# Graph attention and feed-forward on one core: SyncE takes two transfers from GpSimd, and GpSimd's gathers are written out with their own waits

## The chip, the cores and the metric

The kernel runs on one core of a Trainium2 chip. The time is what the device needs for one execution, in microseconds (us), as the median of several runs. The core has five engines that run their own instruction streams and wait for each other by semaphores: TensorE (PE, with its weight loads as PEld), VectorE (DVE), ScalarE (ACT), GpSimd (POOL) and SyncE (SP). SP only issues DMAs; POOL issues DMAs too, among them the indirect ones that gather rows by index.

## The reference, cut to what matters

```
x: 12500 x 256;  src, dst: 212500 edges, sorted by dst (100000 each way and 12500 self loops)
x = x + gnn(layernorm(x), edges)
  gnn: h = x @ W (4 heads of 64);  alpha = leaky_relu(a_src[src] + a_dst[dst])
       alpha = softmax of alpha over the edges of each dst
       out = relu(layernorm(sum over edges of alpha * h[src] + bias))
x = x + ffn(layernorm(x))
  ffn: router on the mean row picks 2 of 8 experts for all rows;
       gelu(x @ W1) @ W2 of the two, weighted, then a layer norm
```

## The kernel before, in words

**Table.** The rows of x are taken in 50 pairs of 128-row blocks. For each pair PE transposes, multiplies with W and the attention vectors, ACT scales, and SP stores 269 values a row into `table` in DRAM (`store_pair`, L516). Beside it POOL gathers 75 groups of 128 rows of x straight from the input (`gather_x`, L712): the source rows of tile 13 of the first 75 edge chunks. It stages them in SBUF and stores them, three groups at a time, as `x_src` (`store_x`, L723). One group in three waits for an older store, since the staging space is a ring.

**Chunk loop.** The edges stand in 119 chunks of 14 tiles of 128. For chunk n POOL gathers the table rows of its source nodes, 128 rows with each indirect DMA (L775), into one of four slots of `rows`. In the first 73 of these steps that is 13 gathers, as tile 13 is computed from `x_src` by PE and ACT (SP loads it as `xe`, L554); in the other 46 it is 14. The indices come through `idx`, four slots, loaded by SP (L539), the first four by POOL (L737). Behind the gathers a chain over all engines computes maxima, weights and messages and adds them up by node. The chain for chunk n begins with ACT's copy of the gathered logits into `asrc` (L1130), followed by PE's matmul "lT" (L888); the two next chunks are gathered meanwhile.

Every engine runs the same step list, `walk`: six steps written out at the start, then loops of four steps. POOL's `walk` has four more written steps where the count of gathers changes.

**Waits.** In each step POOL waits until the slot's old content has been used: for `idx`, for ACT ("msgs") and DVE (the last message), and for PE ("expand*"). Before the seventh gather (t = `FIRST_ROW` = 6) it waits for PE's "lT^" of an earlier chunk. The last wait of each group is carried by a 1x1 `tensor_tensor` on `turn` (L768, L774), which also counts `s_turn`; in the x phase a `tensor_tensor` on `x_turn` (L711) does the same. `hold` is a semaphore increment that carries a wait of its own.

**Feed-forward.** After the last chunk the two experts are loaded and 25 groups of rows pass through PE, ACT and DVE. POOL is idle there.

The order of all this is written by hand; no scheduler sets it. The functions that the change touches, with the lines of the profile:

Of the kernel before, what the change touches and what calls it, by code (L numbers as in the profile page):

```python
# [128 lines left out]
def build(nc, x, src_t, dst, W, att_src, att_dst, g_bias, g_gamma, g_beta, Wr, br, W1, b1, W2, b2,  # L129
# [29 lines left out]
    with ExitStack() as ctx:  # L159
        def sb(name, shape, dt=F32):  # L160
            return ctx.enter_context(nc.sbuf_tensor(name, shape, dt))

        def sem(name):
            return ctx.enter_context(nc.semaphore(name))
# [37 lines left out]

        spare = sb("spare", [1, TILES], I32)
        turn = sb("turn", [1, 3])
        x_turn = sb("x_turn", [1, X_CHUNKS])
# [119 lines left out]
        s_wide = sem("s_wide")  # L325
        s_narrow = sem("s_narrow")
        s_dst16 = sem("s_dst16")
        s_first_idx = sem("s_first_idx")
# [4 lines left out]
        s_xidx = sem("s_xidx")  # L333
        s_xrow = [sem(f"s_xrow{i}") for i in range(RING - 1)]
        s_xsrc = [sem(f"s_xsrc{i}") for i in range(RING - 1)]
        s_xe = [sem(f"s_xe{i}") for i in range(2)]
        s_mid = sem("s_mid")
        s_fwr = sem("s_fwr")
# [90 lines left out]
        def hold(eng, counted):  # L429

            eng.sem_inc(counted, 1)  # L431

        def walk(eng, total, step, long=False, late=0):
            for j in range(-4, 2):
                step(At(0, RING, j), -j, 5)

            def four(k, late=RING):
                for j in range(RING):  # L440
                    step(At(k, RING, j + 2), -2, 5 if j < late else 2)

            with nc.Fori(0, X_ROUNDS, engines=[eng.engine], hint_back_edge=long) as k:
                four(k)
            hold(eng, s_nested)
            if late:
                four(X_ROUNDS, late)
            with nc.Fori(X_ROUNDS + (late > 0), SURE, engines=[eng.engine], hint_back_edge=long) as k:
                four(k, 0)
            hold(eng, s_nested)  # L450
            with eng.If(total > SURE * RING + 3):
                with eng.Fori(SURE, (STEPS - 3) // RING, WALK) as far:
                    with eng.If(far * RING + 3 < total):
                        with nc.Fori(far, far + WALK, engines=[eng.engine], hint_back_edge=long) as k:
                            with eng.If(k * RING + 3 < total):
                                four(k, 0)
                        hold(eng, s_nested)

        def among(lo, hi):

# [6 lines left out]
        def each_pair(begin, end):  # L467

            return [At(p // PAIR_RING, PAIR_RING, p % PAIR_RING) for p in range(begin, end)]

        def stored_x(eng):

            for i in range(RING - 1):
                eng.wait_ge(s_xsrc[i], 16 * len(x_parts[i::RING - 1]))
                hold(eng, s_nested)

        def rows_landed(at, lead, hi):

# [11 lines left out]
        def _(sp):  # L490
# [103 lines left out]
            hold(sp, s_sp_held)  # L594
            sp.dma_start(dst16[0:P * EP].rearrange("(p e) -> p e", p=P), narrow).then_inc(s_dst16, 16)
            pairs(SCHED_AT[1], PAIRS // PAIR_RING * PAIR_RING)
            for at in each_pair(PAIRS // PAIR_RING * PAIR_RING, PAIRS):
                pair(at, False)
            store_pair(each_pair(PAIRS - 1, PAIRS)[0], 0)
            total = steps_to_run(sp)  # L600
            sp.wait_ge(s_dst16, 16)
            hold(sp, s_sp_held)
            for j in range(2):
                load_dst(j, sp.value_load(step_tab[0:1, 1, j:j + 1], min_val=0, max_val=chunks - 1))
            for j in range(PAIR_RING):
                sp.wait_ge(s_tab[j], 16 * (len(range(j, PAIRS, PAIR_RING)) + 1))
                sp.wait_ge(s_x[j], 16 * len(range(j, LOADED, PAIR_RING)))
# [70 lines left out]
        def _(pool):  # L678
# [18 lines left out]
            def stage(c):  # L697
                c %= x_ring * X_BATCH
                return (c // X_SLOT + 1) * slot_size + c % X_SLOT * D

            def gather_x(c):

                i, r = divmod(c, X_BATCH)
                if r == 0 and i >= x_ring:
                    j = i % (RING - 1)
                    pool.wait_ge(s_xsrc[j], 16 * len(range(j, i - 1, RING - 1)))
                    hold(pool, s_granted)
                if c > 1:
                    pair_of = (c - 2) * 2 // 3
                    p1_pe.wait(pool, "T*", each_pair(pair_of, pair_of + 1)[0])  # L710
                    pool.tensor_tensor(x_turn[:, c:c + 1], zeros[0:1, 0:1], zeros[0:1, 0:1], ALU.add)  # L711
# [3 lines left out]
                if r == X_BATCH - 1 and i > 0:  # L715
                    store_x(i - 1)

            def store_x(i):

                j, part = i % (RING - 1), x_parts[i]  # L720
                pool.wait_ge(s_xrow[j], 16 * sum(p.stop - p.start for p in x_parts[j:i + 1:RING - 1]))
                hold(pool, s_granted)
                pool.dma_start(x_src.rearrange("(q i) d -> q (i d)", i=X_CHUNKS)[:, part.start * D:part.stop * D],  # L723
                               flat_rows[:, bass.ds(stage(part.start), (part.stop - part.start) * D)])\
                    .then_inc(s_xsrc[j], 16)

            pool.wait_ge(s_xidx, 16)
            for c in range(X_CHUNKS // 3):
                gather_x(c)
            pool.wait_ge(s_wide, 16)  # L730
            pool.tensor_scalar(narrow, wide, float(TOP16), None, ALU.min).then_inc(s_narrow, 1)
            for c in range(X_CHUNKS // 3, X_CHUNKS - 6):
                gather_x(c)
            total = steps_to_run(pool)
            for j in range(RING):
                c = pool.value_load(step_tab[0:1, 1, j:j + 1], min_val=0, max_val=chunks - 1)
                pool.dma_start(idx[j][:, :], src_t[bass.ds(c * P, P), :]).then_inc(s_first_idx, 16)  # L737
            for c in range(X_CHUNKS - 6, X_CHUNKS):
                gather_x(c)
            store_x(len(x_parts) - 1)  # L740
            pool.wait_ge(s_first_idx, 16 * RING)
            for j in range(RING):
# [5 lines left out]
            def gather(at, lo, hi):  # L748

                slot = at.slot(1)  # L750
                if not among(lo, hi)[3]:
                    return
                if at.off + 1 == 1:
                    stored_x(pool)
                pool.wait_ge(s_idx[slot], at.landed(1, 1))
                hold(pool, s_granted)
                first_row = lo == 1
                if not first_row:
                    act2.wait(pool, "msgs", at, -3)
                    hold(pool, s_granted)  # L760
# [1037 lines left out]
```

## Time and profile before

| | |
|---|---|
| median of 3 runs | 2975.58 us (2974.57 to 2977.32) |
| the profiled execution's own time | 2978.09 us |
| its span | 2976.4 us |
| mean granted clock of PE over the span | 0.86 |
| PE busy | 2415.0 us, 81% |
| DVE busy | 2279.3 us, 77% |
| ACT busy | 1725.7 us, 58% |
| POOL busy | 1694.2 us, 57%, of it 1524.3 in 1593 table gathers (L775), 957 ns each |

Busy time leaves out register, branch and semaphore instructions. The span is what the profiler saw from the first to the last instruction; the execution's own time is a little longer. In a row of the timeline the number in square brackets is the idle time of the engine before the instruction, and what ended it; "issue" is time in which it waited for nothing that the profile shows. An engine's share of the whole span says little here, since the stages have different limits.

### The profile page before, as it was taken

Reading aid. Unit: us, or ns where it says so; the run is one execution under the profiler, and the core shown is the slowest. Engines: PE = TensorE matmul, PEld = TensorE weight load, DVE = VectorE, ACT = ScalarE, POOL = GpSimd, SP = SyncE. Lnnn points to the kernel's source line nnn. Section 1 sums busy time; section 2 is a strip of 40 time slices with the busy share of each in tenths; the row PEclk is TensorE's granted clock in tenths of the full one; section 3 lists DMA queues with packets and bytes.
Section 4 is the critical chain, followed back from the end, with each engine's and each line's share of the span. In section 5 each row is a group of like instructions: output and inputs, shape, how many; then the busy total and the mean of one; then the engine's idle time right before and its main releaser. Section 6 shows DMA issues by size and latency. Waiting matters only on the chain. (4 is left out here: it accounts for less than half of the span.)

```text
span 2976.4 us, 67870 instructions
## 1 busy us (share of the span) xinstructions
PE 2415.0 (81%) x13182; PEld 1788.0 (60%) x13182; DVE 2279.3 (77%) x9533; ACT 1725.7 (58%) x5721; POOL 1694.2 (57%) x2041
## 2 busy tenths in 40 slices
PE   7927788888888888887777766777767999999998
PEld 6725566666666666665555555555554666667666
DVE  5638888988989989988888888888875565665655
ACT  4627777777777778777666666666662121221221
POOL 6777777777777777777777777777740000000000
PEclk9959888887878888878777787777778999999999
DMA  8966565656666655665555555555541111101101
GB/s 280 358 180 170 165 174 167 174 167 172 169 170 171 172 168 171 170 169 166 159 162 159 159 156 157 160 160 160 157 113 43 43 36 35 43 29 43 43 28 39
DMA packets 237752, 417.88 MB, mean 140 GB/s; under 512 B 68257, under 2 KB 153121, under 8 KB 237537
## 3 DMA queue, kind: packets, MB, share of 16 engines
q0 software_dynamic: 82640, 239.20, 30.3%
q1 hardware_dynamic: 153546, 175.16, 18.1%
q10 hardware_dynamic: 1351, 1.63, 0.2%
q14 instruction: 200, 1.64, 0.2%
q8 instruction: 15, 0.25, 0.0%
HBM read 362.57 MB, written 53.26 MB: 140 GB/s over the span
## 5 line engine op out<-in xcount | busy, mean ns | idle before, releaser
L775 POOL DMA_INDIRECT rows<-table,idx x1593 | 1524.3, 957 | 448.9 <-issue 386.4
L868 PE MATMUL bank<-msg,oh 128*128 128x260 f32 x3332 | 967.8, 452 | 2.2 <-ACT acc L1144 2.2
L868 PEld LDWEIGHTS bank<-msg,oh 128*128 128x128 f32 x3332 | 757.7, 232 | 147.5 <-DVE r_d L1492 2.6
L1098 ACT ACTIVATE msg<-rows,we 128x65 f32<-128x65 f32 x1904 | 478.5, 333 | 0.4
L916 PE MATMUL bank<-ident_b,ohT 128*128 128x128 bf16 x1680 | 190.0, 300 | 322.3 <-ACT oh L1091 126.5
L1398 DVE TENSOR_TENSOR msg<-rows,bank 128x520 f32<-128x520 f32 x595 | 382.7, 678 | 1.0 <-DVEq L110 0.8
L916 PEld LDWEIGHTS bank<-ident_b,ohT 128*128 128x128 bf16 x1680 | 159.8, 139 | 340.6 <-ACT oh L1091 201.2
L1233 ACT ACTIVATE msg<-bank,b_sb 128x512 f32<-128x512 f32 (+1 forms) x200 | 134.4, 678 | 365.5 <-PE bank L972 347.7
L985 PE MATMUL bank<-rows,msg 128*128 128x256 f32 x1536 | 340.6, 378 | 0.0
L972 PE MATMUL bank<-rows 128*128 128x512 f32 x768 | 335.5, 594 | 4.3 <-DMA rows<-in_L_ffn_W 4.3
L985 PEld LDWEIGHTS bank<-rows,msg 128*128 128x128 f32 x1536 | 288.4, 189 | 51.4 <-issue 10.6
L972 PEld LDWEIGHTS bank<-rows 128*128 128x128 f32 x768 | 146.0, 190 | 179.6 <-issue 175.5
L1118 ACT ACTIVATE carry<-bank 1x265 f32<-1x265 f32 x118 | 45.1, 382 | 311.2 <-PE bank L941 309.5
L1091 ACT ACTIVATE oh_b<-bank 128x896 bf16<-128x896 bf16 x238 | 205.3, 914 | 20.6 <-ACTq L110 15.6
L1091 ACT ACTIVATE oh<-bank 128x896 f32<-128x896 bf16 x238 | 200.7, 890 | 0.3 <-ACTq L110 0.2
L1393 DVE TENSOR_SCALAR ohT<-dst_b,node 128x896 bf16<-128x896 int16 x240 | 161.9, 674 | 8.0 <-DVE mtile L1511 7.4
L1500 DVE TENSOR_REDUCE node_v<-bank 128x70 f32<-128x210 f32 x119 | 44.5, 374 | 157.7 <-PE bank L888 157.5
L1669 DVE TENSOR_TENSOR rows<-bank,msg 128x512 f32<-128x512 f32 x49 | 31.6, 686 | 140.6 <-PE bank L985 137.6
L1180 ACT ACTIVATE selfm<-tab_w,ws 128x65 f32<-128x65 f32 x476 | 127.0, 338 | 3.9
L888 PE MATMUL bank<-ident,asrc 128*70 128x128 f32 x240 | 51.8, 298 | 94.7 <-ACT asrc L1130 78.7
L1148 ACT ACTIVATE r_c<-carry,r_f 1x65 f32<-1x65 f32 x476 | 125.0, 333 | 0.0
L1233 ACT ACT_TABLE_LOAD x12 | 15.4, 1283 | 183.3 <-PE bank L972 183.3
(223 smaller groups left out, 3957.3 us busy)
## 6 DMA issues: line engine op xcount, KB each, us to landing
dst_b<-dst SPq DMA_DIRECT2D x122, 448.0 KB
rows<-table,idx POOLq DMA_INDIRECT x1593
tab_w<-table SPq DMA_DIRECT2D x121, 134.5 KB
x_w<-in_x_rows SPq DMA_DIRECT2D x121, 128.0 KB
x_mid<-x_o SPq DMA_DIRECT2D x119, 128.0 KB
table<-msg SPq DMA_DIRECT2D x50, 269.0 KB, 5.2
rows<-x_mid SPq DMA_DIRECT2D x26, 512.0 KB, 3.5
msg<-in_x_rows SPq DMA_DIRECT2D x51, 256.0 KB
```

The costliest lines, as they stand in the source:

```text
L775: pool.indirect_dma_start(rows[:, slot, t, :], None, table, bass.IndirectOffsetOnAxis(ap=idx[slot][:, t:t + 1], axis=0), bounds_check=None ...
L868: mm = pe.matmul(psA, oh[:, of, t, :], msg[:, of, t, :], start=(t == 0), stop=(t == TILES - 1))
L916: mm = pe.transpose(ps[:, c:c + P], ohT[:, s, t, 0:P], ident_b[:, :])
L972: mm = pe.matmul(u, w1_sb[:, e, k, fk * P:(fk + 1) * P], fxT[:, at.slot(), k, :], start=(k == 0), stop=(k == KD - 1))
L985: mm = pe.matmul(psY[q // 2][:, q % 2, :], hT[:, f, q * P:(q + 1) * P], w2_sb[:, e, fk, :], start=(f == 0), stop=(f == 2 * KF - 1))
L1091: ins = act.activation(to[:, i * half:(i + 1) * half, :], psO[i].rearrange("p (t n) -> p t n", n=P), ACT.Copy)
L1098: ins = act.activation(head_cols(msg[:, s, t, :])[:, h, :], head_cols(rows[:, at.slot(), t, 0:HC1])[:, h, :], ACT.Copy, scale=we[:, t, h:h ...
L1148: ins = act.activation(head_cols(r_c[:, :])[:, h, :], head_cols(carry[:, 0:HC1])[:, h, :], ACT.Copy, scale=r_f[:, h:h + 1])
L1180: ins = act.activation(head_cols(selfm[:, :])[:, h, :], head_cols(tab_w[:, at.slot(), 0:HC1])[:, h, :], ACT.Copy, scale=ws[:, h:h + 1])
L1233: act3.mark(HID[f], act.activation(hT[:, f, 0:n], psU[f % len(psU)][:, 0:n], ACT.Gelu, bias=b1_sb[:, e, fk:fk + 1]))
L1393: return dve.tensor_scalar(ohT[:, s, t, 0:P], dst_b[:, s, :].rearrange("p (t n) -> p t n", n=P)[:, t, :], node[:, s:s + 1], None, ALU.is_e ...
L1398: mark(own, name, lambda: dve.tensor_tensor(msg[:, s, t:t + 2, :].rearrange("p t (h c) -> p t h c", h=H), rows[:, s4, t:t + 2, 0:HC1].rear ...
```

## The change

- SP, not POOL, loads the first four `idx`: right behind the loop over the pairs of blocks, before the last three table stores.
- SP, not POOL, stores the last three groups of x rows (semaphore `s_xlast`), behind the first loads of dst.
- POOL's `tensor_tensor` on `turn` and `x_turn` go. The gather behind it carries the wait itself.
- POOL's steps are written out one by one (`for n in range(-4, SURE * RING + 2)`), so that the values waited for are constants. Only steps beyond the first 119, which this input does not need, stay in a loop, with `turn` as before (`repeated`).

The other engines keep `walk`; its form with four written steps is gone, which only POOL used.

```diff
         def stored_x(eng):
             for i in range(RING - 1):
-                eng.wait_ge(s_xsrc[i], 16 * len(x_parts[i::RING - 1]))
+                eng.wait_ge(s_xsrc[i], 16 * len(x_parts[:-1][i::RING - 1]))
                 hold(eng, s_nested)
+            eng.wait_ge(s_xlast, 16)
+            hold(eng, s_nested)
...
             pairs(SCHED_AT[1], PAIRS // PAIR_RING * PAIR_RING)
+            total = steps_to_run(sp)
+            for j in range(RING):
+                c = sp.value_load(step_tab[0:1, 1, j:j + 1], min_val=0, max_val=chunks - 1)
+                sp.dma_start(idx[j][:, :], src_t[bass.ds(c * P, P), :]).then_inc(s_idx[j], 16)
             for at in each_pair(PAIRS // PAIR_RING * PAIR_RING, PAIRS):
                 pair(at, False)
             store_pair(each_pair(PAIRS - 1, PAIRS)[0], 0)
-            total = steps_to_run(sp)
...
                 load_dst(j, sp.value_load(step_tab[0:1, 1, j:j + 1], min_val=0, max_val=chunks - 1))
+            for j in range(RING - 1):
+                sp.wait_ge(s_xrow[j], 16 * sum(p.stop - p.start for p in x_parts[j::RING - 1]))
+            sp.dma_start(*x_rows_out(x_parts[-1])).then_inc(s_xlast, 16)
...
                     p1_pe.wait(pool, "T*", each_pair(pair_of, pair_of + 1)[0])
-                    pool.tensor_tensor(x_turn[:, c:c + 1], zeros[0:1, 0:1], zeros[0:1, 0:1], ALU.add)
...
-            for c in range(X_CHUNKS // 3, X_CHUNKS - 6):
+            for c in range(X_CHUNKS // 3, X_CHUNKS):
                 gather_x(c)
             total = steps_to_run(pool)
-            for j in range(RING):
-                c = pool.value_load(step_tab[0:1, 1, j:j + 1], min_val=0, max_val=chunks - 1)
-                pool.dma_start(idx[j][:, :], src_t[bass.ds(c * P, P), :]).then_inc(s_first_idx, 16)
-            for c in range(X_CHUNKS - 6, X_CHUNKS):
-                gather_x(c)
-            store_x(len(x_parts) - 1)
-            pool.wait_ge(s_first_idx, 16 * RING)
-            for j in range(RING):
-                pool.sem_inc(s_idx[j], 16)
...
-                if at.off > -1:
-                    pool.wait_ge(s_turn, at.k * (2 * RING) + 2 * (at.off + 1))
+                if repeated:
+                    pool.wait_ge(s_turn, at.k * (2 * RING) + 2 * (at.off + 1 - SURE * RING - 2))
                     hold(pool, s_granted)
                 if not first_row:
                     pe2.wait(pool, "expand*", at, -3)
-                pool.tensor_tensor(turn[:, 0:1], turn[:, 2:3], turn[:, 2:3], ALU.add).then_inc(s_turn, 1)
+                if repeated:
+                    pool.tensor_tensor(turn[:, 0:1], turn[:, 2:3], turn[:, 2:3], ALU.add).then_inc(s_turn, 1)
...
-                        pool.tensor_tensor(turn[:, 1:2], turn[:, 2:3], turn[:, 2:3], ALU.add).then_inc(s_turn, 1)
+                        if repeated:
+                            pool.tensor_tensor(turn[:, 1:2], turn[:, 2:3], turn[:, 2:3], ALU.add).then_inc(s_turn, 1)
...
-            walk(pool, total, gather, late=2)
+            for n in range(-4, SURE * RING + 2):
+                first_steps = n < X_ROUNDS * RING + 4
+                gather(At(0, RING, n), -n if n < 2 else -2, 5 if first_steps else 2)
+            pool.sem_inc(s_turn, 2)
+            far_rounds(pool, total, lambda at, lo, hi: gather(at, lo, hi, repeated=True))
```

How this orders the instructions is seen in three places. First POOL before, where the x phase ends (`x_src<-rows` are the stores of x rows, `rows<-table` the gathers of the chunk loop; "waits" names the semaphores):

```order
L736 TENSOR_LOAD step_tab
L736 ISA x2
L737 ISA
L737 DMA idx<-in_src_tiles 128x14
L711 TENSOR_TENSOR x_turn<-zeros 1x1 [waits s_xsrc2,p1_pe]
L712 DMA rows<-in_x_rows,oh 128x256
L723 DMA x_src<-rows 128x768 [waits s_xrow2]
L723 DMA x_src<-rows 128x768 [waits s_xrow0]
L768 TENSOR_TENSOR turn<-turn 1x1 [waits s_first_idx,s_dst16,s_tab3,s_idx0,s_tab2,s_tab0,s_tab1]
L775 DMA rows<-table,idx 128x269 x6
```

And POOL in the changed kernel, at the same place:

```order
L722 DMA rows<-in_x_rows,oh 128x256 [waits s_xsrc0,p1_pe]
L722 DMA rows<-in_x_rows,oh 128x256 [waits p1_pe] x2
L733 DMA x_src<-rows 128x768 [waits s_xrow2]
L495 TENSOR_LOAD tot_i [waits s_setup]
L495 ISA x2
L776 DMA rows<-table,idx 128x269 [waits s_dst16,s_tab3,s_idx0,s_tab2,s_tab0,s_tab1]
L776 DMA rows<-table,idx 128x269 x12
```

The four index DMAs with their loads and the last store are gone from POOL; one load of the total stands before the first gather. On SP, at the end of the table's pairs, the changed kernel has the loads before the last three table stores:

```order
L495 TENSOR_LOAD tot_i [waits s_setup]
L495 ISA x2
L608 TENSOR_LOAD step_tab
L608 ISA x2
L609 ISA
L609 DMA idx<-in_src_tiles 128x14
L525 DMA table<-msg 128x538 [waits p1_act] x3
L616 TENSOR_LOAD step_tab [waits s_dst16]
```

where the kernel before had

```order
L516 DMA table<-msg 128x538 [waits p1_act] x3
L486 TENSOR_LOAD tot_i [waits s_setup]
L486 ISA x2
L604 TENSOR_LOAD step_tab [waits s_dst16]
L604 ISA x2
```

The load of the entry and the index DMA stand there four times. One step of the chunk loop on POOL before, inside the loop:

```order
L103 REGISTER_ALU [waits s_idx0]
L103 REGISTER_ALU [waits act2]
L764 REGISTER_ALU [waits dve2]
L103 REGISTER_ALU [waits s_turn]
L768 TENSOR_TENSOR turn<-turn 1x1 [waits pe2]
L775 DMA rows<-table,idx 128x269 x6
L103 REGISTER_ALU
L774 TENSOR_TENSOR turn<-turn 1x1 [waits pe2]
L775 DMA rows<-table,idx 128x269 x8
```

and now:

```order
L776 DMA rows<-table,idx 128x269 [waits s_idx0,act2,dve2,pe2]
L776 DMA rows<-table,idx 128x269 x5
L776 DMA rows<-table,idx 128x269 [waits pe2]
L776 DMA rows<-table,idx 128x269 x7
```

The registers, the two tensor_tensors and the wait for `s_turn` are gone; the first and the seventh gather carry waits.

## Rows read from the trace of the kernel before

**Rows 1.** Busy time by stretch; counts in brackets, granted clock, DMA share, GB/s.

```profile
330.00:1372.00 1042.00, 862.57 (x5408) 667.75 (x5408) 931.59 (x4144) 809.41 (x2896) 809.45 (x944) 0.82 0.61 170
1372.00:2191.00 819.00, 582.24 (x3717) 442.68 (x3715) 676.70 (x2968) 551.64 (x1852) 635.52 (x738) 0.79 0.58 159
```

**Rows 2.** View of line L1130; windows 164 to 330, 330 to 1372, 1440 to 2191.

```profile
L1130 ACT ACTIVATE asrc<-rows x9: 266/266/268, 182.5 to 315.7; 128x70 f32<-128x70 f32 x9
...
  DMA rows<-table,idx: 31.3, 9
...
L1130 ACT ACTIVATE asrc<-rows x63: 247/249/266, 332.4 to 1361.2; 128x70 f32<-128x70 f32 x63
...
  DMA rows<-table,idx: 63.2, 42
```

**Rows 3.** Timeline (start, length, engine, line), POOL and ACT, 1105 to 1115 us.

```profile
1105.38 1.20 POOL L775 DMA_INDIRECT rows<-table,idx  x1 [0.30 <-issue]
...
1113.76 0.25 ACT L1130 ACTIVATE asrc<-rows 128x70 f32<-128x70 f32 x1
...
1114.59 0.18 POOL L774 TENSOR_TENSOR turn<-turn 1x1 f32<-1x1 f32 x1 [0.43 <-PE bank L888]
```

**Rows 4.** POOL by line, 1372 to 2191, then L768 in 164 to 1372 us.

```profile
L775 POOL DMA_INDIRECT rows<-table,idx x645 | 614.5, 953 | 182.3 <-issue 154.3 <-DVE mnode L1525 8.8 <-ACT r_f L1140 1.8
L768 POOL TENSOR_TENSOR turn<-turn 1x1 f32<-1x1 f32 x46 | 11.9, 259 | 0.7
L774 POOL TENSOR_TENSOR turn<-turn 1x1 f32<-1x1 f32 x46 | 9.4, 204 | 0.8
...
L768 POOL TENSOR_TENSOR turn<-turn 1x1 f32<-1x1 f32 x72 | 13.6, 188 | 1.2
```

**Rows 5.** Timeline of POOL around one L768.

```profile
1513.46 0.95 POOL L775 DMA_INDIRECT rows<-table,idx  x1 [0.30 <-issue]
1514.42 0.21 POOL L768 TENSOR_TENSOR turn<-turn 1x1 f32<-1x1 f32 x1
1514.78 0.96 POOL L775 DMA_INDIRECT rows<-table,idx  x1
```

**Rows 6.** Timeline of POOL at the start of the gathers.

```profile
142.01 0.59 POOL L723 DMA_DIRECT2D x_src<-rows  x1
...
149.67 1.02 POOL L712 DMA_INDIRECT rows<-in_x_rows,oh  x1 [0.16 <-issue]
...
163.09 0.56 POOL L723 DMA_DIRECT2D x_src<-rows  x1 [3.66 <-DMA rows<-in_x_rows,oh]
...
164.44 1.02 POOL L775 DMA_INDIRECT rows<-table,idx  x1 [0.50 <-issue]
```

**Rows 7.** DMA issues of POOL (KB each, median us from issue to landing).

```profile
x_src<-rows POOLq DMA_DIRECT2D x25, 384.0 KB, 5.9
```

**Rows 8.** Timeline of SP from the last table stores to xe.

```profile
143.40 0.34 SPq L516 DMA_DIRECT2D table<-msg  x1
...
149.98 0.33 SPq L516 DMA_DIRECT2D table<-msg  x1
...
152.56 1.03 SPq L542 DMA_DIRECT2D dst_s<-dst  x1
...
159.82 0.34 SPq L550 DMA_DIRECT2D tab_w<-table  x1
...
167.95 8.61 SPq L554 DMA_DIRECT2D xe<-x_src  x4
```

**Rows 9.** View of table; landing of its stores, 120 to 200 us.

```profile
DMA to landing us min/median/max: 2.8/5.5/6.2
```

**Rows 10.** Timeline of ACT, its last work before asrc of chunk 0.

```profile
176.92 0.20 ACT L1204 ACTIVATE xln<-xln 128x1 f32<-128x1 f32 x1
```

**Rows 11.** DMA queues (packets, MB, share) while POOL runs the x phase, 18 to 164 us.

```profile
q14 instruction: 8, 0.07, 0.1%
q8 instruction: 2, 0.03, 0.1%
```

More of the change, by code:

```diff
@@ L204, in build @@
         turn = sb("turn", [1, 3])
-        x_turn = sb("x_turn", [1, X_CHUNKS])
         idx = [sb(f"idx{i}", [P, TILES], I32) for i in range(RING)]
@@ L327, in build @@
         s_dst16 = sem("s_dst16")
-        s_first_idx = sem("s_first_idx")
         s_idx = [sem(f"s_idx{i}") for i in range(RING)]
@@ L335, in build @@
         s_xsrc = [sem(f"s_xsrc{i}") for i in range(RING - 1)]
+        s_xlast = sem("s_xlast")
         s_xe = [sem(f"s_xe{i}") for i in range(2)]
@@ L431, in hold, with four, far_rounds @@
             eng.sem_inc(counted, 1)
[L435 to L439, printed above, removed]
-                for j in range(RING):
[L441 to L450, printed above, removed]
+        def four(k, step, hi):
+            for j in range(RING):
+                step(At(k, RING, j + 2), -2, hi)
+        def far_rounds(eng, total, step, long=False):
             with eng.If(total > SURE * RING + 3):
@@ L455, in walk @@
                             with eng.If(k * RING + 3 < total):
-                                four(k, 0)
+                                four(k, step, 2)
                         hold(eng, s_nested)
+        def walk(eng, total, step, long=False):
+            for j in range(-4, 2):
+                step(At(0, RING, j), -j, 5)
+            with nc.Fori(0, X_ROUNDS, engines=[eng.engine], hint_back_edge=long) as k:
+                four(k, step, 5)
+            hold(eng, s_nested)
+            with nc.Fori(X_ROUNDS, SURE, engines=[eng.engine], hint_back_edge=long) as k:
+                four(k, step, 2)
+            hold(eng, s_nested)
+            far_rounds(eng, total, step, long)
         def among(lo, hi):
@@ L469, in each_pair, with stage, x_rows_out @@
             return [At(p // PAIR_RING, PAIR_RING, p % PAIR_RING) for p in range(begin, end)]
+        def stage(c):
+            c %= x_ring * X_BATCH
+            return (c // X_SLOT + 1) * slot_size + c % X_SLOT * D
+        def x_rows_out(part):
+            return (x_src.rearrange("(q i) d -> q (i d)", i=X_CHUNKS)[:, part.start * D:part.stop * D],
+                    flat_rows[:, bass.ds(stage(part.start), (part.stop - part.start) * D)])
         def stored_x(eng):
             for i in range(RING - 1):
-                eng.wait_ge(s_xsrc[i], 16 * len(x_parts[i::RING - 1]))
+                eng.wait_ge(s_xsrc[i], 16 * len(x_parts[:-1][i::RING - 1]))
                 hold(eng, s_nested)
+            eng.wait_ge(s_xlast, 16)
+            hold(eng, s_nested)
         def rows_landed(at, lead, hi):
@@ L596, in _ @@
             pairs(SCHED_AT[1], PAIRS // PAIR_RING * PAIR_RING)
+            total = steps_to_run(sp)
+            for j in range(RING):
+                c = sp.value_load(step_tab[0:1, 1, j:j + 1], min_val=0, max_val=chunks - 1)
+                sp.dma_start(idx[j][:, :], src_t[bass.ds(c * P, P), :]).then_inc(s_idx[j], 16)
             for at in each_pair(PAIRS // PAIR_RING * PAIR_RING, PAIRS):
@@ L695, in _ @@
             pool.memset(rows[:, :, GATHERS, :], 1.0).then_inc(s_pool, 1)
-            def stage(c):
-                c %= x_ring * X_BATCH
-                return (c // X_SLOT + 1) * slot_size + c % X_SLOT * D
             def gather_x(c):
@@ L714, in gather_x @@
                                         bounds_check=None, oob_is_err=False).then_inc(s_xrow[i % (RING - 1)], 16)
-                if r == X_BATCH - 1 and i > 0:
+                if c == x_parts[i].stop - 1 and i > 0:
                     store_x(i - 1)
@@ L722, in store_x @@
                 hold(pool, s_granted)
-                pool.dma_start(x_src.rearrange("(q i) d -> q (i d)", i=X_CHUNKS)[:, part.start * D:part.stop * D],
-                               flat_rows[:, bass.ds(stage(part.start), (part.stop - part.start) * D)])\
-                    .then_inc(s_xsrc[j], 16)
+                pool.dma_start(*x_rows_out(part)).then_inc(s_xsrc[j], 16)
             pool.wait_ge(s_xidx, 16)
@@ L731, in _ @@
             pool.tensor_scalar(narrow, wide, float(TOP16), None, ALU.min).then_inc(s_narrow, 1)
-            for c in range(X_CHUNKS // 3, X_CHUNKS - 6):
+            for c in range(X_CHUNKS // 3, X_CHUNKS):
                 gather_x(c)
             total = steps_to_run(pool)
-            for j in range(RING):
-                c = pool.value_load(step_tab[0:1, 1, j:j + 1], min_val=0, max_val=chunks - 1)
-                pool.dma_start(idx[j][:, :], src_t[bass.ds(c * P, P), :]).then_inc(s_first_idx, 16)
-            for c in range(X_CHUNKS - 6, X_CHUNKS):
-                gather_x(c)
-            store_x(len(x_parts) - 1)
-            pool.wait_ge(s_first_idx, 16 * RING)
-            for j in range(RING):
-                pool.sem_inc(s_idx[j], 16)
             for j in range(PAIR_RING):
@@ L746, in _, with gather @@
             pool.wait_ge(s_dst16, 16)
-            def gather(at, lo, hi):
+            def gather(at, lo, hi, repeated=False):
                 slot = at.slot(1)
```

## The prediction, made before the changed kernel ran

> **What bounds the kernel now.** I read the totals first, then the stretches, then who waits in each, then single rows at the boundaries. By its total of 57% POOL is no bottleneck. But the program has three stages. Before 164 us it builds the table; to 2191 us it runs 119 steps over edge chunks; then comes the feed-forward part, in which POOL has nothing to do. In the chunk loop POOL is busy 809 of 1042 us and 636 of 819 us [rows 1]. The rest is no free time: between two gathers lie 0.30 us whose releaser is "issue", so a gather of 0.95 us takes 1.25 us of POOL [rows 5].
>
> Whether POOL is the bound is seen at its consumer. The first instruction of a step that needs the gathered rows is ACT's copy into asrc (L1130). In the first nine steps it waits for them 31.3 us; in the 63 steps from 330 to 1372 us it never does; in the 42 steps from 1440 us on it does every time, 63.2 us in all [rows 2]. So there are three regimes. Steps 0 to 8 are POOL-bound. In the middle the compute chain paces itself: 332.4 to 1361.2 us in 62 intervals is 16.59 us a step [rows 2], at a granted clock of 0.82 [rows 1]. The consumer falls behind there, until asrc stands 7.2 us behind the end of its gathers (1113.76 against 1105.38 + 1.20), and then it is POOL that waits, 0.43 us at L774 for PE's matmul behind asrc [rows 3]. From chunk 73 on a step has 14 gathers instead of 13, and POOL is the bound again to the end of the loop, while ACT has 63.2/42 = 1.5 us of idle in each step. The stage after it hangs on the last gather.
>
> **The change part by part.**
>
> 1. The two 1x1 tensor_tensors of each step go (L768, L774). One costs POOL less than its body, because it takes the place of an issue gap: 0.01 us from the gather's end to L768, 0.21 for L768, 0.15 to the next gather, against 0.30 without it [rows 5]. In the last regime the two kinds take (11.9 + 9.4)/92 = 0.232 us with (0.7 + 0.8)/92 = 0.016 idle before [rows 4]. So each costs 0.232 + 0.016 + 0.15 - 0.30 = 0.098 us, and 92 of them 9.0 us. POOL sets the pace there, and ACT's 1.5 us of slack is far more than the 0.2 us a step that go, so all 9.0 us come through. Early a tensor_tensor is shorter (0.188, [rows 4]) and the same sum gives 0.054. The middle regime makes nothing of it, since the consumer paces there. The first nine steps have 18: 1.0 us.
>
> 2. In the middle regime POOL only gets ahead, to the same limit of 7.2 us, where it waits for PE. With 0.11 us a step less it touches that limit in each of the consumer's slow phases and enters the last regime with more lead. I take six steps' worth, 0.7 us; bounds 0 and 1.5 us.
>
> 3. The waits now sit on the gathers themselves. No row shows an indirect gather whose own wait is satisfied. The nearest is L723, POOL's other DMA, which carries a wait and starts without a gap (142.01, [rows 6]). From below, the gap before the gather could be the 0.15 us that lies behind a tensor_tensor: -0.15 x 92 = -14 us. From above it could be the 0.50 us before the first table gather [rows 6], which stands behind a wait that held: +0.20 x 92 = 18 us. I take 0.30, no cost: the semaphore instructions between a gather and L768, four of them, took 0.01 us [rows 5], so waits are passed while the gather before still runs.
>
> 4. The start of the gathers. After the store at 142.01 POOL loads a total and four table entries and issues four index DMAs until 149.67; the last of its stores waits 3.66 us for x rows, and gather 0 starts at 164.44 [rows 6]. Changed, it has six x gathers, two stores and one load left. The last three x gathers need the store of 142.01 landed, which takes 5.9 us [rows 7], so they start at 147.9; three gathers are 3.8 us, a store 0.6, a load 1.1 (below): POOL is ready near 153.5.
>
>    What is late next is the table. SP stores pairs at 143.40 and 149.98 and two between them. The change puts a total, four entries and four DMAs behind the first. Two loads took 152.56 - 150.31 = 2.25 us, 1.1 each, and a DMA 0.34 [rows 8]: 5 x 1.1 + 4 x 0.34 = 6.9 us. From 143.74, SP thus comes to the second store at 150.6 and to the last at 151.8, 1.8 us later than now. A table store lands after 2.8 to 6.2 us, median 5.5 [rows 9]: 157.3. With 0.5 us to restart, gather 0 begins at 157.8 instead of 164.44: 6.6 us. What is queued on SP behind: the load of dst for two chunks, whose start hardly moves since the total has been read; the last x store near 157, which must land before gather 1 at 157.8 + 13 x 1.25 = 174.1 and does; the windows, at 159.82 behind ACT's padding of x_mid; and xe at 167.95 [rows 8], unchanged. ACT ends the x work that stands before asrc of chunk 0 at 177.1 [rows 10], against 182.5 now [rows 2], so chunk 0 gains 5.4 us at most, but chunk 1 and all behind it gain the 6.6. Bounds: 3 us (SP and landing both late) and 9.5 us (table no later than now).
>
> 5. The 73 x_turn tensor_tensors go. They are inside the 153.5 above and worth nothing by themselves while the table is later.
>
> 6. POOL's two loops become written steps. Price zero: its x gathers and first three chunks are straight-line code already. While it ran 75 gathers and 25 stores in 146 us, the two queues of instruction loads moved 8 and 2 packets for all engines [rows 11], and the gathers ran on at 1.3 us. By the Trainium skill (Runtime: NRT & Kernel Launch, Instruction fetch mechanics) sequential code is fetched ahead and its loading mostly hidden, while a taken branch can force a load. By that rule unrolling might even win something; L768 and the rows around it show no such gap at POOL's back edges.
>
> Sum: -6.6 - 1.0 - 0.7 - 9.0 = -17.3 us. From the profiled execution (2978.09, its span 2976.4 and 1.7 us around it) that gives 2960.8. The median of the runs shown is 2.5 us lower, 2975.58, and 17.3 less is 2958.3: I forecast 2958.
>
> **The rivals.**
>
> A. A wait on a gather costs what the tensor_tensor did, 0.098 us: the 9.0 us stay, total -8.3, 2967. At the 0.20 us bound it is -17.3 + 18, no change. For it: the new form is in no row. Against: four waits cost 0.01 us in front of L768.
>
> B. The start gains only 3 us: SP's loads take longer, or three table stores close together land late among x rows and padding. -13.7, 2962.
>
> C. What lengthens the tensor_tensors late in the loop, 259 ns against 188 [rows 4], is VectorE's access to SBUF, and the gathers inherit it. Then only the short part goes: 92 x 0.054 = 5.0 us instead of 9.0, total -13.3, 2962. Against it: the gathers' own late mean is 953 ns [rows 4], no longer than a single one. The Trainium skill names such a mechanism (SBUF — State Buffer, the note "The DVE blocks DMA trap"): a DMA whose descriptors POOL generates is locked out while certain VectorE instructions hold a shared port.
>
> D. The other side: the written-out code is not loaded in time. In the x phase there was at most one packet for each ten of POOL's DMAs [rows 11], so the 644 gathers of the last regime need at most 64. If each held POOL up by the 0.50 us of a restart, that is 32 us against 17 won: +15, 2990. It turns to a loss from 17.3/64 = 0.27 us a packet. Against it is the even spacing in today's straight-line part.
>
> E. More than forecast: the table no later than now (9.5), the lead regained in full (1.5), and a gap under 0.30 on some gathers: -24, 2951.
>
> **How the numbers follow.** Forecast 0.52, A 0.12 (a third of it near no change), B 0.12, C 0.09, D 0.05, E 0.10. A measurement of this kernel can tell a change from none at about 0.2%, 6 us. Faster by more than that are the forecast, B, C, E and most of A: 0.87 with a little taken off; within it 0.08; slower 0.05. The range, 2949 to 2969, takes in E, B, C and A, and leaves out D and the dear form of A.
>
> **What would show it right or wrong.** Gather 0 between 155 and 160, released by the last table store. Gaps before gathers with waits of 0.30 us as before those without; 0.4 or more is A, and a mean spacing above 1.26 us without waits is C or D. The middle regime must keep 16.6 us a step with more waiting of POOL for PE than now. The last regime must fall from 819/46 = 17.8 [rows 1] to 17.6 us a step. The forecast is wrong if the middle regime changes its pace, or if ACT no longer waits for gathers behind 1440 us.

## The result, and the profile after

| us | before | changed |
|---|---|---|
| median | 2976.36 (2974.57 to 2977.54, 5 runs) | 2963.36 (2962.04 to 2971.48, 5 runs) |
| the profiled execution's own time, its span | 2978.09, 2976.4 | 2971.48, 2969.7 |
| the five spans of the changed kernel | | 2969.7, 2961.4, 2961.1, 2963.2, 2960.1 |

The ratio is 0.9961 with an interval of 0.9950 to 0.9972: 11.6 us faster (8 to 15), where 17.3 were forecast. The trace is that of the longest of the five executions, 6.7 us under the span of before. At 2971.48 us it lies above the forecast's range; what the others won beyond it has no trace.

The start first. Timeline of the changed kernel, SP and POOL (start, length, engine, line; in brackets the idle time before and what ended it); it answers to [rows 6, 8]:

```profile
148.81 2.03 SPq L525 DMA_DIRECT2D table<-msg  x3
...
150.42 0.58 POOL L733 DMA_DIRECT2D x_src<-rows  x1
...
157.74 0.35 SPq L619 DMA_DIRECT2D x_src<-rows  x1
158.43 0.97 POOL L776 DMA_INDIRECT rows<-table,idx  x1 [7.42 <-DMA table<-msg]
...
167.87 8.64 SPq L563 DMA_DIRECT2D xe<-x_src  x4
...
175.87 0.95 POOL L776 DMA_INDIRECT rows<-table,idx  x1 [1.43 <-PEq L110]
```

POOL is done with its x work at 151.0 and then waits 7.4 us for the table's last stores; gather 0 starts 6.0 us earlier than before. But chunk 1's gathers, the row at 175.87, carry a wait for PE, whose x work hangs on xe, and xe is loaded when it was before. They begin 1.1 us later than POOL could.

ACT's copy into asrc, the consumer, in chunk 1, before (first fence) and changed:

```profile
198.91 0.27 ACT L1130 ACTIVATE asrc<-rows 128x70 f32<-128x70 f32 x1 [8.90 <-DMA rows<-table,idx]
```

```profile
193.88 0.27 ACT L1135 ACTIVATE asrc<-rows 128x70 f32<-128x70 f32 x1 [8.82 <-DMA rows<-table,idx]
```

So 5.0 us are won at chunk 1. View of L1135 of the changed kernel in 164 to 330, 330 to 1372 and 1440 to 2184 us, against [rows 2]:

```profile
L1135 ACT ACTIVATE asrc<-rows x10: 248/266/268, 177.5 to 329.7; 128x70 f32<-128x70 f32 x10
...
  DMA rows<-table,idx: 23.3, 5
...
L1135 ACT ACTIVATE asrc<-rows x62: 248/249/253, 346.8 to 1360.6; 128x70 f32<-128x70 f32 x62
...
  DMA rows<-table,idx: 49.2, 39
```

Now only five early steps wait for gathers. Chunk 71 is read at 1360.6, before at 1361.2: of the 5.0 us, 0.6 are left. Its 61 intervals from 346.8 us are 16.62 us each, against 16.59 before. Part of the loss can be placed. Before's windows (first fence) and the changed kernel's, of 263 to 280, 280 to 297 and 297 to 314 us; the number before the DMA share is PE's granted clock:

```profile
263.00:280.00 17.00, 13.14 (x88) 9.90 (x87) 14.86 (x68) 12.97 (x47) 13.14 (x17) 0.90 0.58 169
280.00:297.00 17.00, 13.59 (x90) 10.24 (x89) 15.33 (x69) 13.34 (x49) 13.32 (x16) 0.90 0.62 172
297.00:314.00 17.00, 12.83 (x94) 9.69 (x92) 14.65 (x66) 14.06 (x51) 13.31 (x16) 1.00 0.62 171
```

```profile
263.00:280.00 17.00, 15.15 (x89) 11.84 (x89) 15.31 (x68) 13.16 (x49) 13.04 (x14) 0.71 0.62 169
280.00:297.00 17.00, 14.14 (x88) 10.93 (x88) 15.06 (x67) 12.90 (x48) 12.73 (x15) 0.80 0.61 172
297.00:314.00 17.00, 14.14 (x88) 10.92 (x87) 15.03 (x67) 13.09 (x47) 13.04 (x14) 0.80 0.60 171
```

Before, PE kept 0.90 to 1.00 from 246 to 314 us; changed, it fell to 0.71 and 0.80 some 50 us sooner, the same chunks cost more, and at chunk 8 the lead was 3.0 us (asrc at 312.68 against 315.7). That the clock is the cause is read from the times, not tested. POOL itself was ahead by more: its gathers of chunk 8 ended at 306.85 against 312.91, 6.1 us earlier, so the 1.0 us forecast for the first nine steps did come on POOL. But POOL does run at its limit of lead: it waits for PE's "lT" 12.6 us in 17 times, where before it waited once, 0.4 us. View of POOL's waits in 330 to 1372 us (waited, times, longest):

```profile
POOL rows L776 <- PE bank L893: 12.6, 17, 0.8
```

The last regime. The stretches, POOL by line, and one gather that carries its step's waits with its neighbour, against [rows 1, 4, 5]:

```profile
330.00:1372.00 1042.00, 862.84 (x5381) 667.13 (x5381) 930.33 (x4138) 809.60 (x2887) 786.44 (x814) 0.82 0.61 169
1372.00:2184.00 812.00, 586.78 (x3717) 446.69 (x3717) 674.89 (x2962) 551.88 (x1851) 615.95 (x645) 0.79 0.58 160
```

```profile
L776 POOL DMA_INDIRECT rows<-table,idx x644 | 615.6, 956 | 196.3 <-issue 181.1 <-DVE mnode L1530 8.5 <-ACT r_f L1145 2.7
```

```profile
1513.29 1.21 POOL L776 DMA_INDIRECT rows<-table,idx  x1 [0.30 <-issue]
1514.81 0.95 POOL L776 DMA_INDIRECT rows<-table,idx  x1 [0.31 <-issue]
```

From the end of chunk 72's gathers to that of the last it takes 811.9 us and not 818.3 (1371.75 to 2183.66; 1372.33 to 2190.61): 17.65 us a step and not 17.79. That is 6.4 us, 0.070 for each of the 92 tensor_tensors. The gap before a gather with waits is 0.30 us. What is longer is the gather itself: the first of a step has a mean of 1.010 us in these 46 steps, the second 0.947. Before, these were 0.966 and 0.950.

The loading of code: queues in 18 to 158 us [rows 11] and over the span, 212 packets in q14 against 200 before, with no gap in the gathers that would go with them:

```profile
q14 instruction: 7, 0.06, 0.1%
q8 instruction: 2, 0.03, 0.1%
```

### The profile page after: what moved, and what is told of

It reads as the page before. It is cut to its first block and busy times, and to the rows that moved or that the text cites. A ratio compares the mean times of both kernels' runs of the same rounds, so it can differ in the third digit from the quotient of the medians.

```text
span 2969.7 us, 66763 instructions
## 1 busy us (share of the span) xinstructions
PE 2424.8 (82%) x13182; PEld 1797.2 (61%) x13182; DVE 2279.2 (77%) x9533; ACT 1729.8 (58%) x5721; POOL 1634.2 (55%) x1725
## 5 line engine op out<-in xcount | busy, mean ns | idle before, releaser
L873 PE MATMUL bank<-msg,oh 128*128 128x260 f32 x3332 | 978.4, 456 | 2.3 <-DVEq L110 2.3
L873 PEld LDWEIGHTS bank<-msg,oh 128*128 128x128 f32 x3332 | 765.0, 234 | 150.8 <-DVE r_d L1497 2.7
L1619 DVE COPY rows<-bank 128x512 f32<-128x512 f32 x50 | 32.2, 686 | 108.5 <-PE bank L962 108.5
```

What stands on the lines that cost most here:

```text
L873: mm = pe.matmul(psA, oh[:, of, t, :], msg[:, of, t, :], start=(t == 0), stop=(t == TILES - 1))
```

## The experiments

All twelve ran on four chips, later than the result. On each of the four the kernel before has a median of 3385 to 3389 us, 14% more than in the result. The changed kernel ran unchanged on two of them, and is not faster there but 2.1 and 2.3% slower. So the experiments could not repeat the 11.6 us, and became a study of why the change loses on chips where a step of gathers takes longer. Times are compared on the chip of each run. "The first chip" is the chip or setting of the result; whether it is one of the four isn't recorded.

| kernel | turn at step start, at 7th gather | us | ratio to before, interval | ACT idle before the carry copy, us |
|---|---|---|---|---|
| before_look | yes, yes | 3395.33 (before: 3387.56) | | 17 |
| start_only | yes, yes | 3390.49 | 1.0001, 0.9992 to 1.0010 | 21 |
| with_turn | yes, yes | 3386.44 | 0.9997, 0.9988 to 1.0007 | 6 |
| first_turn | yes, no | 3383.38 | 0.9995, 0.9985 to 1.0004 | 9 |
| second_turn | behind the first gather | 3448.71 | 1.0172, 1.0151 to 1.0193 | 332 |
| lt_turn | no, yes | 3466.05 | 1.0230, 1.0199 to 1.0260 | 398 |
| again | no, no | 3464.59 | 1.0229, 1.0211 to 1.0248 | 384 |
| after_look | no, no | 3462.96 | 1.0213, 1.0200 to 1.0227 | 378 |
| written_only | no, no | 3461.10 | 1.0219, 1.0206 to 1.0232 | 376 |
| all_wait | no, no | 3456.41 | 1.0226, 1.0199 to 1.0252 | 368 |
| spaced | no, no, spacers | 3411.27 | 1.0079, 1.0063 to 1.0096 | 179 |
| lead12 | no, no, wait at 13th | 4069.25 | 1.2007, 1.1991 to 1.2022 | 1089 |

The last column is the sum of the releasers' rows, as in the fences below, for the copy PE -> ACT of `carry` in 330 to 2600 us. It compares kernels on these chips alone: on the first chip it is 302 us before and 311 changed, nearly all of it released by the product itself, since ACT is there early and waits for PE.

**again.** The changed kernel, unchanged.

> The changed kernel itself, for a second profile and the spread of its times. In the first profile (2971 us) gather 0 began 6.0 us earlier but the start of the last regime (end of chunk 72's gathers) came only 0.6 us earlier, because the middle regime took 16.64 us a step in cycles of 8 steps instead of 16.58 in cycles of 7. Theory 1 (the middle regime's pace is set by how the granted clock falls on the steps, differently from run to run): times of 2961 to 2966 us, and a second profile near 2963 shows cycles of 7 steps and a last regime that begins about 6 us earlier. Theory 2 (the lost start is a property of the changed kernel): the same cycles of 8 steps again, and the 8 us between profile and median lie elsewhere.

Measured: 3464.59 us against 3388.43, 2.3% slower, and so not what the result on the first chip says. Neither theory can be judged by it; where the other four executions of the result won their further 6.5 to 9.6 us stays open.

**start_only and written_only.** The change in two parts. start_only has only the transfers moved to SP, with loops and tensor_tensors as before; written_only has only the other part.

```diff
 start_only, against the changed kernel
-            for n in range(-4, SURE * RING + 2):
...
+            walk(pool, total, gather, late=2)
...
 written_only, against the changed kernel
-            for c in range(X_CHUNKS // 3, X_CHUNKS):
+            for c in range(X_CHUNKS // 3, X_CHUNKS - 6):
```

> Only the two transfers move to SP; loops, tensor_tensors on turn and x_turn as before. Theory 1 (the start is worth what chunk 1 gains, about 5 us): 0.9983 of before, 2971 us. Theory 2 (the middle regime eats the start): 0.9995 to 1.0005. Both expect gather 0 near 158.5 to 160 us and a last regime of 17.79 us a step as before.

> Only the written-out steps with the waits on the gathers, without tensor_tensors; first indices and last x rows stay with POOL. Theory 1 (the last regime gains 46 x 0.14 to 0.2 us, and the rest adds): 0.9970 to 0.9978, about 2969 us, the last regime at 17.65 us a step, gather 0 at 163 to 164.5. Theory 2 (the whole gain of 12 us is that of the loop and the start is worth nothing): 0.9960.

On these chips the start is worth nothing and the other part is the whole loss. In start_only's trace gather 0 begins at 164.2 us and not at 168.2 (before_look, another of the four), but chunk 1's first gather at 190.0 and not at 188.2: the start's lead is gone within one chunk.

**with_turn.** The changed kernel with both tensor_tensors and the wait for s_turn back.

```diff
...
-                if repeated:
-                    pool.tensor_tensor(turn[:, 0:1], turn[:, 2:3], turn[:, 2:3], ALU.add).then_inc(s_turn, 1)
+                pool.tensor_tensor(turn[:, 0:1], turn[:, 2:3], turn[:, 2:3], ALU.add).then_inc(s_turn, 1)
```

(and the same for `turn[:, 1:2]`)

> The changed kernel with the tensor_tensors on turn put back in front of the waits' gathers (and the wait for s_turn); steps still written out with constant waits, x_turn still gone, start as changed. Theory 1 (the tensor_tensors are the cost in the loop): the last regime at 17.79 us a step, 6 to 9 us more than the changed kernel, 0.9983 of before. Theory 2 (registers and branches were the cost): as the changed kernel, 0.996, and 17.65 us a step.

No loss: the written-out code costs nothing here either. It is the missing tensor_tensors, or the missing wait for s_turn, that cost 78 us (3464.6 against 3386.4). The wait alone is ruled out below: lt_turn and second_turn have it and lose all the same.

**before_look and after_look.** Both kernels' traces on one of these chips.

> The kernel before, unchanged, for a profile on the chip on which the others of this set run. If this is the slower chip (3388 us), theory S (what the changed kernel loses there is a wait that really blocks: the seventh gather of a step waits for lT, and started from a wait a gather comes later than a tensor_tensor does) expects its middle steps to be 19.9 us long with spacings of 3.07 us at the first gather and 2.98 us at the seventh, as the kernel with only the start changed had, and tensor_tensors that begin 1.7 us after PE has written lT. If it is the first chip (2976 us), the profile repeats the one shown: middle steps of 16.6 us, last ones of 17.79 us, hardly any wait for lT.

> The changed kernel again. On the slower chip: 2.2% slower than before, as in the first set (3465 against 3388 us), middle steps of 21.1 us. On the first chip: ratio 0.996 (11 to 12 us faster), chunk 1's gathers 5 us earlier, middle steps 16.6 us, last ones 17.65 us. Theory P (the loss belongs to one loading of the program, not to the chip) would allow 2.2% to be absent at the slower chip this time.

Timeline of POOL, before:

```profile
1239.65 0.95 POOL L775 DMA_INDIRECT rows<-table,idx  x1 [0.30 <-issue]
1240.90 0.95 POOL L775 DMA_INDIRECT rows<-table,idx  x1 [0.30 <-issue]
1243.59 0.18 POOL L768 TENSOR_TENSOR turn<-turn 1x1 f32<-1x1 f32 x1 [1.74 <-remote]
1243.92 1.07 POOL L775 DMA_INDIRECT rows<-table,idx  x1
```

and changed:

```profile
1204.39 0.94 POOL L776 DMA_INDIRECT rows<-table,idx  x1 [0.30 <-issue]
1210.13 0.95 POOL L776 DMA_INDIRECT rows<-table,idx  x1 [4.79 <-PE bank L893]
...
1217.70 0.95 POOL L776 DMA_INDIRECT rows<-table,idx  x1 [0.30 <-issue]
1220.69 0.95 POOL L776 DMA_INDIRECT rows<-table,idx  x1 [2.04 <-remote]
```

In both, POOL stands 1.7 to 2.1 us before most gathers that are under a wait ("remote" is a releaser that the profile can't name). The exception is the changed kernel's seventh gather in the middle regime: 3.2 us in the median, and 4.79 in the row at 1210.13. Without waits a gather takes 1.25 us as on the first chip. The mean step before is 19.96 us for 13 gathers and 21.36 for 14, which is 1.53 us a gather both times. The changed kernel has 21.35 in the last regime, the same, but 21.09 in the middle, where its seventh gather comes 4.17 us after the sixth (before: 2.98). The whole loss is made before the last regime: chunk 72's gathers end at 1699.0 us against 1621.0.

**lt_turn and lead12.** The tensor_tensor back before the seventh gather alone; and the wait for lT moved to the 13th.

```diff
-        FIRST_ROW = 6
+        FIRST_ROW = 12
```

> The changed kernel with one tensor_tensor of the two put back in each step: that before the seventh gather, which then carries the wait for lT. On the slower chip, theory S expects nearly the whole loss gone: the seventh gather's spacing back from 4.18 to 2.98 us and the time within 0.3% of before (3385 to 3400 us), though the first gather of a step still carries its waits; theory Q (each gather that carries a wait costs the same, wherever it is) expects half of it, 3425 us. On the first chip, where POOL is the engine that bounds the last regime, it costs 0.05 to 0.10 us in each of 46 steps, 2 to 5 us more than the changed kernel.

> The changed kernel with the wait for lT before the 13th gather of a step and not before the seventh, so that POOL may run 7.5 us further ahead. On the slower chip, theory S expects the wait for lT to be satisfied nearly always, the 1.2 us per middle step to go and perhaps more: 3370 to 3400 us. If the loss comes from the phase that POOL falls into and not from the blocked wait, it stays near 3465. On the first chip: POOL no longer waits for lT (12.6 us in 17 waits before), the middle regime is held by the chain of the other engines either way, so at most 3 us faster than the changed kernel; last regime the same 17.65 us a step.

Theories S and Q both fell. The blocked seventh gather isn't the cause, since a tensor_tensor there leaves the time at 3466 us; and a POOL that may run further ahead made the kernel 20% slower. Timeline of lead12 (PE, POOL, SP, ACT, DVE):

```profile
1195.37 0.61 PE L946 MATMUL bank<-acc,sel 128*1 128x265 f32 x2
...
1203.75 0.95 POOL L776 DMA_INDIRECT rows<-table,idx  x1 [0.30 <-issue]
1206.92 0.33 SPq L563 DMA_DIRECT2D xe<-x_src  x1
1206.92 0.38 ACT L1123 ACTIVATE carry<-bank 1x265 f32<-1x265 f32 x1 [13.07 <-remote]
1207.34 0.14 DVE L1482 TENSOR_SCALAR r_t<-carry 1x1 f32<-1x1 f32 x1 [10.19 <-ACT carry L1123]
```

ACT's copy of PE's product `carry` waits for nothing but PE, which is done at 1196.0. It starts 10.9 us later, 2.2 us after POOL's twelfth gather in a row has ended, and SP issues the load of xe in the same instant. In 46 steps from 300 to 1500 us this handoff, start to start, has a median of 11.31 us, in the kernel before here 0.85 and on the first chip 0.65. So on this chip a signal between two other engines is held up while POOL issues twelve gathers back to back, and gets through when POOL pauses. With six or seven in a row the kernel before shows 0.85 us, so a row of gathers alone doesn't do it. That became theory B in the expectations below: the descriptors of the gathers pile up.

The traces settle the pile itself. They hold every packet that the DMA engines moved, and each table gather has 48. View of lead12's DMA queues from 1205.0 to 1206.9 us, where the packets of the twelfth gather lie:

```profile
DMA packets 48, 0.14 MB, mean 73 GB/s; under 512 B 16, under 2 KB 16, under 8 KB 48
q0 software_dynamic: 48, 0.14, 26.1%
```

They run from 1205.40 to 1206.24. The first starts 1.65 us behind the start of their gather; for the first of the row, at 1189.85, it is 1.64. Counted off in the same way, the first packet comes 1.6 to 2.4 us behind its gather on average at every place in a step, in before and after as in before_look and after_look. Eleven gathers with 0.28 us of backlog each would have made it 3 us later. So the transfers do not pile up on the slower chips, and theory B's cause is refuted; that signals pass late is what is left of it.

**first_turn.** The other tensor_tensor alone, at the start of the step.

> The changed kernel with the other one of the two tensor_tensors put back in each step: that at the step's start, not that before the seventh gather. With both back the loss is gone (ratio 0.9997), with only the second back it isn't (1.023). If the loss hangs on the start of a step, this one is at 1.000; if it needs both, at 1.02. Theory B (below) says only that the phase of the step decides, and gives no number here.

The loss is gone with this one. View of the carry copy, in 330 to 2600 us, of first_turn and of after_look (idle before it, times, by releaser):

```profile
  issue: 7.0, 9
  remote: 1.1, 1
  PE bank L947: 1.1, 2
```

```profile
  remote: 162.5, 35
  PE bank L873: 124.0, 28
  PE bank L880: 73.2, 35
  issue: 15.0, 4
  PE bank L946: 3.3, 3
```

By the code the copy waits for the product `carry` alone (L946, L947 in first_turn); L873 and L880 are PE's products that end nearest to its late start. Every kernel without a tensor_tensor at the step's start has 179 us or more here, every kernel with one 21 or less (table).

**spaced and all_wait.** A 1x128 tensor_tensor before each gather that has no wait; or a wait for a constant on each of those.

```diff
+                    if not repeated and t not in (0, FIRST_ROW):
+                        ins = pool.tensor_tensor(spacer[:, t, :], zeros[0:1, 0:128], zeros[0:1, 0:128], ALU.add)
...
+                    if t not in (0, FIRST_ROW):
+                        pool.wait_ge(s_const, 6)
```

> The changed kernel with a tensor_tensor of 1x128 before each of the 11 or 12 gathers of a step that carry no wait, so that gathers come 1.4 to 1.55 us apart and not 1.25. Theory B (backlog): on this chip the descriptors of a gather take 1.53 us to get away, however they are issued (19.96 us / 13 and 21.36 us / 14 in both kernels), the 1.7 to 2.2 us before the first and seventh gather are the backlog of the ones before, and signals of other engines pass late while there is one. It expects the pauses at the first and seventh gather to shrink from 1.7 to under 1 us, steps no longer than 20.0 and 21.4 us, and the changed kernel's loss gone or nearly: 3380 to 3410 us. Theory F (a wait on GpSimd costs 1.7 us by itself on this chip) expects the pauses unchanged and each step longer by 11 times the spacer, 2 us or more: 3600 us or more.

> The changed kernel with a wait for a value that has stood since the start on each gather that had none. Theory F (1.7 us for each wait) expects 11 x 1.7 = 19 us more in each of 119 steps: 5600 us. Theory B expects a wait to cost only what the backlog is at that moment, 0.28 us a gather: spacings of 1.53 us throughout, pauses of at most 0.6 us, and no more than the changed kernel's 3465 us, with 3390 likely. On the first chip, where no backlog shows, both expect spacings of 1.25 to 1.3 us.

Spaced, timeline of POOL with a step's start at 1254.56:

```profile
1250.86 1.00 POOL L784 DMA_INDIRECT rows<-table,idx  x1 [0.16 <-issue]
1251.88 0.39 POOL L781 TENSOR_TENSOR spacer<-zeros 1x128 f32<-1x128 f32 x1
1252.42 0.97 POOL L784 DMA_INDIRECT rows<-table,idx  x1 [0.16 <-issue]
1254.56 0.95 POOL L784 DMA_INDIRECT rows<-table,idx  x1 [1.17 <-remote]
```

A spacer adds 0.28 us to each of 11 or 12 gathers, 3.1 us a step or more, and the step of the last regime stays at 21.33 us, the middle one falls from 21.09 to 20.32. The pauses shrink: the first gather comes 1.30 us after the one before it in the last regime (3.18 before), the seventh 1.29 (3.09). Theory F, a fixed price of a wait, is refuted, and the last regime's pace of 1.53 us a gather holds with spacers as without. It does not hold in every kernel: lead12's middle steps take 26.4 us, 2.03 a gather. The time, 3411 us, is just above B's range: two thirds of the loss are gone, not all.

all_wait refutes F once more, and B's number too. Gathers with a satisfied wait, timeline:

```profile
1212.11 0.95 POOL L778 DMA_INDIRECT rows<-table,idx  x1 [0.30 <-DVE adsh_p L1561]
1213.36 1.01 POOL L778 DMA_INDIRECT rows<-table,idx  x1 [0.30 <-issue]
1214.67 0.95 POOL L778 DMA_INDIRECT rows<-table,idx  x1 [0.30 <-issue]
```

They come every 1.25 us as without it, where B had expected 1.53: a wait for a value that has long stood costs nothing. By this, what POOL stands for at its two pauses is the late arrival of a signal, not the wait.

**second_turn.** first_turn with its tensor_tensor moved behind the step's first gather.

```diff
-                pool.tensor_tensor(turn[:, 0:1], turn[:, 2:3], turn[:, 2:3], ALU.add).then_inc(s_turn, 1)
...
+                    if t == 1 and not repeated:
+                        pool.tensor_tensor(turn[:, 0:1], turn[:, 2:3], turn[:, 2:3], ALU.add).then_inc(s_turn, 1)
```

> The kernel with one tensor_tensor a step (first_turn) with that tensor_tensor moved behind the step's first gather: the gather carries the step's waits, as in the changed kernel, and the same 1x1 tensor_tensor stands before the second gather, with no wait of another engine on it. Theory C (what costs the slower chip 2.2% is that the step's waits sit on a gather) expects 1.020 to 1.023, 3455 us or more, middle steps of 21 us, and ACT's copy of the carry, 0.8 us after PE's product in the good kernels, again 5 to 6 us after it. Theory D (a tensor_tensor near the start of a step is enough, by the 0.1 to 0.15 us that it puts between gathers) expects 0.998 to 1.003, 3380 to 3395 us and middle steps of 19.9 us.

1.0172, middle steps of 20.80 us, 332 us of idle before the carry copy, and the copy 4.3 us behind the product in the median: theory D is refuted. C's signs are there, with a handoff and a loss a little under what it had said (1.72% against 2.0 to 2.3). Standing near the start of the step is not enough: of the kernels tried, those with a tensor_tensor in front of the first gather, where it carries the step's waits, don't lose.

No version beats both kernels on these chips: first_turn is at 0.9995 of before, which the interval does not tell from 1. It was not run on the first chip, where it would cost, as an estimate from the 6.4 us for both, half of that: some 3 us in the last regime.

## Why the prediction was right or wrong

The forecast (2958, 2949 to 2969) holds the measured 2963.4, and the change is faster. Of its sum of 17.3 us, 11.6 came. The number came out better than the mechanism: in the trace the start and the last regime, forecast at 6.6 and 9.0 us, are worth 0.6 and 6.4, and the rest of the 11.6 came in executions that nobody traced. That the median fell into the range is in part luck. By its own steps, in the profiled execution (first chip):

- **Step 1, the tensor_tensors: mis-sized.** 6.4 us in the last regime, not 9.0. The sum took all of the late tensor_tensor's 0.232 us as gone. Its lengthening, (259 - 188) = 71 ns at the step's start, went over in part to the gather in its place: 1.010 us where the step's first gather before had 0.966. That is 0.044 in 46 steps, 2.0 of the 2.6 us that are missing. It goes rival C's way; C's total for the regime was 5.0. C's cause, DVE's access, isn't shown: the long gather at 1513.29 ran beside a row of DVE's small instructions, and no run changed these.
- **Steps 1 and 2 in the middle regime: the failed step.** That the consumer paces there was right (16.62 us against 16.59). But the sum let a lead won before it, 6.6 + 1.0 us, through to the end: "chunk 1 and all behind it gain the 6.6". A stretch in which the compute chain is the bound passes a lead on only if the chain itself starts earlier and keeps its pace. It started 5.0 us earlier and lost 4.4 by chunk 71, 2 of them by chunk 8, where the granted clock fell sooner. POOL's own lead of 6.1 us at chunk 8 then went into 12.6 us of waits for PE's lT, to 0.6 at chunk 72. The other four executions have spans 6.5 to 9.6 us shorter, so in these some of it was probably kept; that wasn't traced. Of step 2's 0.7 us nothing can be told apart from this 0.6.
- **Step 3, waits on gathers: right here, and the step that fails elsewhere.** The gap stayed 0.30 us and rival A is refuted. all_wait shows that a satisfied wait is free on another chip as well. But the step priced only POOL's own time. On the later chips every kernel whose first gather carries the step's waits has late signals between other engines and loses 1.7 to 2.3% (with spacers 0.8, in lead12 20), and neither the sum nor a rival has such a mechanism.
- **Step 4, the start: near.** 158.43 against 157.8, the table released it, SP's last x store came at 157.74 as said. What was missed is the wait of chunk 1's gathers for PE, which hangs on xe, one of the times that step 4 itself found unchanged: 5.0 us, not 6.6.
- **Steps 5 and 6: right.** Rival D is refuted by the first trace and by with_turn, which has the same written-out code and is at 0.9997.

Only the two parts together were measured on the first chip. That the start is worth 5.0 us at chunk 1 and the last regime 6.4 is read from its trace, not shown by a run.

## What to carry to other kernels

Follow a lead stage by stage: won before a stage that another chain paces, it counts only as far as that chain starts earlier, and at the clock that it is then granted. Price a removed instruction by what its engine does in its place, stretch included, not by its whole length. And when an engine issues software gathers back to back, look at handoffs between the *other* engines too: a tiny instruction that takes the waits in front of the first gather can be worth more than its time.

## What the runs showed of the hardware that was not expected

- The same kernel takes 2976 us in one setting and 3385 to 3389 on four chips in another. The gathers' own length is the same (957 and 960 ns on average), and so is their spacing where none waits, 1.25 us. With the pauses before waits the kernel before comes to 1.27 us a gather on the first chip and 1.53 on the others.
- On those, a signal from PE to ACT took 0.85 us in the median (steps from 300 to 1500 us) with 6 or 7 gathers in a row behind a tensor_tensor, 5.8 without one, 11.3 with 12 in a row. On the first chip it took 0.65 in both kernels.
- Which path is shared, and why a gather that waits differs from a tensor_tensor that waits before it, stays open. It is no backlog of transfers: the first packet of a gather moves 1.6 to 2.4 us behind its start on the first chip and on the others. Why spacers dissolve the pauses, and why the last regime keeps 1.53 us a gather with them, stays open too.
